# Asking for one ScalarE function table by name ahead of the softplus steps of a Mamba block with an FP4 feed-forward

## The reference

```python
xz = x @ W_in; x_proj, z = jnp.split(xz, 2, axis=-1)
x_conv = silu(conv(x_proj, conv_w) + conv_b)
ssm = x_conv @ W_xproj                       # 33 numbers for each token
delta = jax.nn.softplus(ssm[..., 0])         # one of them
Bm, Cm = ssm[..., 1:17], ssm[..., 17:]
h_mean = jnp.einsum('bld,bln->bdn', x_conv, delta[..., None] * Bm) / L
y = (jnp.einsum('bdn,bln->bld', h_mean, Cm) + D * x_conv) * silu(z)
x = layernorm(x + y @ W_out)
g, u = fp4_linear(x, w_gate), fp4_linear(x, w_up)
x = layernorm(x + fp4_linear(silu(g) * u, w_down))
```

## Time and profile before

| | |
|---|---|
| time, median of 3 runs | 2242.16 us (2240.13 to 2244.68) |
| span of the profiled execution | 2238.9 us |
| TensorE busy | 2002.6 us, 89% of the span |
| VectorE busy | 1754.4 us, 78% |
| ScalarE busy | 1149.2 us, 51% |
| GpSimd busy | 1108.9 us, 50% |
| softplus steps | 32, with 3 table loads of 1283 ns each |

### The profile page before, as it was taken

The page is one execution under the profiler, slowest core; times in us unless marked ns, Lnnn a source line. Parts: engine busy times, 40 slices in busy tenths (PEclk is TensorE's granted clock), DMA queues, the critical chain, the costliest instruction groups (busy, mean ns, idle before and its releaser), DMA issues.

```text
span 2238.9 us, 37879 instructions
## 1 busy us (share of the span) xinstructions
PE 2002.6 (89%) x10532; PEld 1581.4 (71%) x10532; DVE 1754.4 (78%) x3548; ACT 1149.2 (51%) x2132; POOL 1108.9 (50%) x1643
## 2 busy tenths in 40 slices
PE   2787899899989999899999999899998999977776
PEld 1554677677777777678876777687776777766665
DVE  6234788788878888698877888698887888788876
ACT  2664555555644555455554565455554556433332
POOL 2222455466545555356544556455553555454543
PEclk9999999999999999999999999999999999999998
DMA  2111011111110111111111111111111111000000
GB/s 78 53 52 43 34 48 47 36 42 48 48 40 29 48 43 44 40 48 41 46 35 39 43 46 41 40 48 34 43 49 39 43 44 39 29 19 20 24 20 15
DMA packets 77087, 90.51 MB, mean 40 GB/s; under 512 B 8880, under 2 KB 59952, under 8 KB 76848
## 3 DMA queue, kind: packets, MB, share of 16 engines
q1 hardware_dynamic: 76848, 87.73, 11.9%
HBM read 37.37 MB, written 16.78 MB: 24 GB/s over the span
## 4 chain that ended last, share of the span: by engine, by line
PE 61%; issue 9%; DVE 6%; ACT 4%; POOL 4%; POOLq 0%; DVEq 0%; ACTq 0%
PE pgu L489 18%; PE pd L489 11%; PE pd L537 7%; PE pa L489 5%; PE pb L489 5%; PE pc L519 4%; PE pc L571 4%; PE pe_ L631 2%; PE pa L559 1%; PE pc L496 1%; POOL hbuf L432 1%; PE pe_ L548 1%; POOL rs L439 1%; DVE hbuf L989 1%; DVE hbuf L835 1%
## 5 line engine op out<-in xcount | busy, mean ns | idle before, releaser
L489 PE MATMUL pgu<-wgu_hi,xqT 128*128 128x512 f32 (+1 forms) x1536 | 426.3, 386 | 0.9 <-issue 0.9
L489 PE MATMUL pd<-wd_hi,hqT 128*128 128x256 f32 (+1 forms) x1536 | 334.4, 299 | 18.6 <-DVE r L1011 15.5
L489 PEld LDWEIGHTS pgu<-wgu_hi,xqT 128*128 128x128 f32 x1536 | 279.1, 189 | 75.7 <-issue 27.6
L537 PE MATMUL pd<-wout,g 128*128 128x256 f32 x1024 | 262.7, 401 | 55.6 <-DVE hqT L979 36.4
L489 PEld LDWEIGHTS pd<-wd_hi,hqT 128*128 128x128 f32 (+1 forms) x1536 | 255.9, 190 | 57.2 <-issue 23.8
L945 DVE SCALAR_TENSOR_TENSOR acc<-xps,cw,acc 128x512 f32<-128x512 f32 x256 | 248.5, 971 | 25.1 <-POOL acc L429 24.4
L418 POOL TENSOR_SCALAR rs<-mv 128x1 f32<-128x1 f32 x128 | 61.5, 480 | 396.7 <-DVE mv L1026 228.9
L537 PEld LDWEIGHTS pd<-wout,g 128*128 128x128 f32 x1024 | 191.0, 197 | 92.6 <-issue 69.4
L740 ACT ACTIVATE hqT<-pe_ 128x512 fp32r<-128x512 f32 x128 | 76.2, 595 | 331.6 <-PE pe_ L631 331.6
L402 POOL TENSOR_TENSOR xv<-xnq,qsx 128x256 f32<-128x256 bf16 x128 | 79.2, 619 | 322.8 <-DVE xnq L838 322.8
L489 PE MATMUL pgu<-wgu_lo,xqT 128*128 128x512 f32 (+1 forms) x768 | 228.1, 378 | 0.0
(11 more groups left out here) (133 smaller groups left out, 4670.0 us busy)
## 6 DMA issues: line engine op xcount, KB each, us to landing
xcr<-xcs SPq DMA_DIRECT2D x128, 256.0 KB, 2.3
xin<-in_L_attn_x_dram SPq DMA_DIRECT2D x32, 512.0 KB, 3.9
xres<-in_L_attn_x_dram SPq DMA_DIRECT2D x128, 128.0 KB, 2.1
out_dram<-outb SPq DMA_DIRECT2D x128, 128.0 KB, 1.7
szr<-in_L_attn_W_in_dram SPq DMA_DIRECT2D x1, 1024.0 KB, 7.4
szr<-in_L_ffn_w_down_dram SPq DMA_DIRECT2D x1, 704.0 KB, 8.6
szr<-in_L_ffn_w_gate_dram SPq DMA_DIRECT2D x1, 640.0 KB, 4.6
szr<-in_L_ffn_w_up_dram SPq DMA_DIRECT2D x1, 640.0 KB, 5.7
```

Of the source, the lines that this page charges most:

```text
L489: mm = pe.matmul(bank, lhsT, rhs, start=(m == 0), stop=(m == len(pairs) - 1))
L537: mm = pe.matmul(pd[:, 0:DM], g[:, (s + 1) % 2, c, j * P:(j + 1) * P], wout[:, c, :], start=(c == 0), stop=(c == NB - 1))
```

## The change

One line is added at the head of `softplus`: it emits a table load of the set that holds both the exponential and the logarithm. Nothing is moved by hand and no semaphore changes.

```diff
@@ -715,6 +715,7 @@
             def softplus(sg):

                 st = sg - 1
+                act.preload_act_table_set("natural_log_exp_and_others")
                 act.wait_ge(ssm_added, 4 * st + 4)
                 at_least(act, d_ready, st)
                 act.activation(sp[:, 0, :], ssm[:, :, 0], ACT.Abs).then_inc(sp_link, 1)
```

## The result

The changed kernel takes 2204.38 us (median of 4 runs, 2203.87 to 2205.99) against 2243.42 us before (4 runs, 2240.13 to 2247.82). The ratio is 0.9828, with a 95% interval of 0.9811 to 0.9846: 1.7% faster. The profiled execution has a span of 2202.1 us against 2238.9, so 36.8 us went.

What follows compares the result with a forecast made beforehand. TensorE, busy 2002.6 of 2238.9 us, was taken as the bound, so ScalarE's time counts only where TensorE waits. 18.3 + 8.0 + 1.4 + 8.3 = 36.0 us off the span gives 2202.9, median 2206 us, range 2199 to 2223.

Steps and rivals of the forecast that it cites:

- ScalarE 1.17 us earlier: From the end of L808 to the start of L740, one load less shortens ScalarE's 4.56 us by 1.17 us.
- No drain: A table load costs 1283 ns on ScalarE without the 1380 ns drain given by the skill page.
- no gain from the wait: Placing the load ahead of ScalarE's wait for `ssm` brings nothing, as there is no wait to hide in.
- Regular steps, 0.90 us each: TensorE's late starts of L537 (0.27 us) and L548 (0.63) vanish in 21 steps, 18.3 us in all.
- the rival of the half gain: Regular steps give 9 us instead of 18.3, as `xv` work meets GpSimd's `g` or another late instruction; 2220 us, chance 0.13.
- Late steps, 1.34 us each: In six steps `dB` ends 0.21 us behind GpSimd's L429, 1.34 us earlier, cutting TensorE's wait before L519; 8.0 us.
- The rival in which GpSimd keeps `dB` out through both: Late steps: `dB` is held through L429 and L432 and ends as before; 2222.5 us, chance 0.07.
- The clock, 8.3 us: L519's matmuls in five of six late steps no longer run partly at the lower clock, 1.66 us each.
- The ends, 1.4 us: First late step gains 1.17 us, the three steps before it nothing, the last one 0.2 us.
- The other falls of the clock: The falls behind L537's 2.4 us wait in the late step were predicted to stay.
- Slower: The named set loads longer than the two it replaces; 2257 us at 3.0 us a load, chance 0.03.
- More than forecast: `dB` slips in ahead of L429, or clock falls elsewhere vanish too; 2196 us, chance 0.02.

Runs made afterwards that it cites:

- the load behind the absolute value: Changed kernel with the named load between softplus's absolute value and exponential instead of ahead of the absolute value; 2201.36 us, ratio 0.9820.
- a fourth load: Changed kernel with two more loads ahead of the absolute value (exponential's own set, named set again), four per softplus; 2284.51 us, ratio 1.0188.
- no loads: Softplus's exponential and logarithm replaced by absolute values and the small Silu left out, so softplus isn't computed and loads no table; 2194.03 us, ratio 0.9787.
- load in the gap: Against the kernel before: named load moved out of softplus to ahead of the copy xqT, where ScalarE waits for TensorE, in every step; 2198.69 us, ratio 0.9809.
- load in the gap late only: Against the changed kernel: named load ahead of the copy xqT in late steps alone, at softplus's head in regular steps; 2193.88 us, ratio 0.9789.

## Why the prediction was right

Forecast 2206.0 us, range 2199 to 2223, measured 2204.38; span forecast 2202.9, measured 2202.1.

*ScalarE 1.17 us earlier.* 1.14 measured (4.56 to 3.42 us). No drain: each load starts 0.02 us behind the activation in front. And no gain from the wait: the load behind the absolute value did as well.

*Regular steps, 0.90 us each.* The mechanism was right, the term was sized low: 0.97. I added the idle times that the timeline prints. They count from the modelled end of the matmul before; L537 now starts 0.17 us before that end (847.40 against 847.57), so the 0.27 of before was a delay of 0.44, and its eight matmuls take 1.89 us, not 1.97. In the other direction, L548 kept 0.18 us of its 0.63: 0.44 + 0.08 + 0.45 = 0.97. VectorE's L836 ran 0.59 us under GpSimd's `g`, the collision that the rival of the half gain named; it was 0.43 us long at that place before, so the collision costs 0.2, not half. Over the 21 steps: 18 x 0.97, and 0.6, 0.8 and 1.0 in the first batch, 19.9 us where 18.3 were forecast.

*Late steps, 1.34 us each.* As forecast: 2.42 to 1.08 in all six, 8.0 us. VectorE got its turn between L429 and L432, and L432 paid 0.12 us for it. The rival in which GpSimd keeps `dB` out through both is refuted.

*The clock, 8.3 us.* Five slow late steps before, none after; on the mean they took 5.24 us and now 3.57, 1.67 us each: 8.3 us. The six late steps of all profiles together say more than those of one: behind a wait of 1.1 us or none 0 of 48 were slow, behind 2.2 to 2.7 us 15 of 24. So the change removed these falls in every profile, but a kernel with the long wait has two to five of them, not five each time, and the term is between 3 and 8 us depending on the execution that one compares with.

*The ends, 1.4 us.* The first late step gave 1.1 us and, not in the sum, the 1.7 us of its own fall of the clock (TensorE's wait went from 3.02 to 1.88 us). The last gave nothing instead of 0.2: there `delta` met L432 and took 1.32 us, and TensorE's wait stayed at 2.90 us.

*What was left out.* TensorE stood 2.6 us longer at the turns of the loop than in the profile before (14.3 against 11.7). The sum is 19.9 + 8.0 + 8.3 + 2.8 - 2.6 = 36.4 of 36.8 us.

The other falls of the clock didn't all stay where they were, as the prediction had assumed. Windows of the profile before, behind L537 in the first of the six late steps and at one turn of the loop, and the same two places after (the granted clock stands behind POOL's column):

```profile
426.70:430.10 3.40, 3.37 (x8) 2.67 (x9) 2.80 (x6) 2.21 (x4) 0.62 (x1) 0.53 0.21 77
904.70:908.10 3.40, 3.38 (x19) 2.94 (x20) 0.23 (x2) 1.10 (x3) 3.06 (x5) 1.00 0.05 12
...
419.00:422.40 3.40, 2.53 (x11) 1.76 (x12) 3.26 (x8) 2.84 (x6) 0.62 (x1) 1.00 0.21 77
888.30:891.70 3.40, 3.40 (x13) 3.07 (x14) 0.69 (x1) 1.20 (x2) 1.66 (x4) 0.53 0.05 14
```

The first is gone after (worth some 0.8 us), and the turns at 888 and 1393 us have a fall that they hadn't before. What those two cost was made up a few microseconds later by shorter waits for VectorE's `xt_lo` and ScalarE's `xcs`: over the five turns, slow matmuls and the waits behind them included, the changed kernel lost 2.5 us, much as the waits at L615 alone say.

*Luck.* The mechanisms were forecast, but that the time lies 1.6 us from the forecast is in part luck. The regular steps gave 1.6 us more and the ends 1.4 us more than their terms, the turns of the loop took 2.6 us back, and the five slow late steps of the profile before are at the upper end of what such a kernel shows.

*Slower.* The load of the named set takes 1283 ns like the others. The slope that the rival used holds for the regular step (1.29 us for a load of 1.28) and not for the late one, where a fourth load cost 0.06 us of waiting.

*More than forecast.* `dB` slipping in ahead of L429 doesn't happen in the changed kernel, but it takes only a logarithm that ends before `hnq` does: three versions have it (no loads, load in the gap, load in the gap late only). With the load behind the absolute value the logarithm ended 0.01 us behind `hnq`, and that was too late. Being ahead of L429 removes the 1.08 us of waiting that were left in each of six late steps.

## What to carry to other kernels

Two functions of ScalarE used in turn can lie in different table sets although one set holds both; then each gets a load, and naming the common set once saves one. What it is worth depends on whether somebody waits at that place: here the third load cost 0.97 us of its 1.28 in a regular step, and the two that are left cost nothing there. Then look at the place: in the late step the load that was left did cost, and put into a gap in which ScalarE waited anyway it no longer held up `dB`. In the regular steps the same gap is 0.1 us too short for it, and there it cost 0.14 us. When a wait is shortened, look at what the late instruction meets at its new time: here another engine's long instruction set the end, and TensorE's clock gave between 3 and 8 us on top of the 8.0 us of the late steps.

## What the runs showed of the hardware

- A VectorE instruction with two inputs in SBUF that starts while GpSimd works on a large tile is held until GpSimd's ends and then ends a fixed time behind it, however early it had started. In the profiles before and after, `dB` (0.36 us alone) ended 0.21 us behind, `delta` (0.16 alone) 0.02, `xv` of L835 (0.43 alone, 128x256) 0.28 and `acc` of L945 (0.75 alone, 128x512) 0.55. `g` of L882, which has one input in PSUM, took 0.75 us in each of the 54 cases in which it started under GpSimd's L429.
- When VectorE was first by 0.11 us, `dB` took 0.36 us and GpSimd's instruction became 0.1 us longer instead. Between two GpSimd instructions that follow each other without a gap VectorE has its turn if its own started before the second one did; `delta` that started 0.01 us behind the second was held through it and took 1.39 us.
- All table loads took 1283 ns and started 0.02 us behind the activation in front, or 0.01 us behind the load in front where two or three stood in a row.
- In the six late steps TensorE's clock was at the lower level behind 15 of 24 waits of 2.2 to 2.7 us, and the eight matmuls took 5.2 to 5.3 instead of 3.57 us; behind 1.1 us in none of 24. The first late step and the last one, at 180 and 1900 us, agree at the ends of the range: slow behind each of nine waits of 2.9 us and more, not slow behind six of 1.7 to 1.9. Between them they don't: six waits of 2.2 to 2.7 us in the last late step brought no fall, so the length of the wait alone doesn't decide it.
